# Second stage of an adaLN block with routed experts: where four quotients, their spreads, the row stores and the low halves are worked

## The reference

```python
h = layernorm(x) * (1 + ca) + sa
x = x + ga * attn(h)            # linear attention, 16 heads of 32
h = layernorm(x) * (1 + cb) + sb
x = x + gb * ffn(h)             # 8 experts, the 2 best of each token

def attn(x):                    # x: 2 x 4096 x 512
    q, k, v = relu(q), relu(k), v         # from x @ w_qkv.T
    vk = einsum('bhen,bhdn->bhed', pad_with_ones(v), k)
    out = einsum('bhed,bhdn->bhen', vk, q)
    out = out[:, :, :-1] / (out[:, :, -1:] + 1e-15)
    return out @ w_proj.T + b_proj
```

## Time and profile before

| what | value |
|---|---|
| time, median of 3 runs | 2205.16 us (2198.65 to 2208.55) |
| profiled execution | 2184.91 us, span 2183.0 us |
| second stage | about 600 to 995 us of the span |
| TensorE busy | 95% of the span |
| VectorE busy | 61% |
| GpSimd, ScalarE busy | 37%, 36% |
| granted clock of TensorE | 0.974 in the mean |

### The profile page before, as it was taken

The page is one execution under the profiler, slowest core; times in us unless marked ns, Lnnn a source line. Parts: engine busy times, 40 slices in busy tenths (PEclk is TensorE's granted clock), DMA queues, the critical chain, the costliest instruction groups (busy, mean ns, idle before and its releaser), DMA issues.

```text
span 2183.0 us, 42591 instructions
## 1 busy us (share of the span) xinstructions
PE 2070.9 (95%) x9416; PEld 1625.2 (74%) x9417; DVE 1322.6 (61%) x3179; ACT 794.0 (36%) x1493; POOL 804.6 (37%) x622
## 2 busy tenths in 40 slices
PE   6999999999979999983999999999999999999997
PEld 4888878888846665662788888888878778888885
DVE  6555564555267888874565656565655555565654
ACT  3444434444345665651222222222222222222222
POOL 4675656566414666653111111111111111111111
PEclk9999999999989999996999999999999999999998
DMA  8666565656545676766855558558775885865554
GB/s 275 241 213 208 168 207 167 207 171 207 183 141 187 228 268 221 275 233 223 238 130 126 129 125 247 124 132 232 181 189 129 264 209 129 237 133 126 130 108 79
DMA packets 293833, 404.89 MB, mean 185 GB/s; under 512 B 50648, under 2 KB 188888, under 8 KB 285920
## 3 DMA queue, kind: packets, MB, share of 16 engines
q1 hardware_dynamic: 166304, 259.74, 37.4%
q0 software_dynamic: 30096, 72.12, 16.0%
q10 hardware_dynamic: 97200, 70.82, 10.3%
HBM read 210.57 MB, written 191.98 MB: 184 GB/s over the span
## 4 chain that ended last, share of the span: by engine, by line
PE 48%; DMA 3%; issue 1%; SPq 1%; ACTq 1%; DVE 0%; ACT 0%; POOL 0%; DVEq 0%; POOLq 0%
PE bank L1753 48%; DMA act_rows<-hact 2%; ACTq L1041 1%; DMA out_rows<-orow,cur_tok 0%; DMA wbuf<-expert_split 0%; SPq L561 0%; DMA expert_rows<-rows,dest 0%; POOL expert_rows L752 0%; DVE x_t_lo L1616 0%; ACT x_t_hi L1023 0%; DVE act_t_lo L1633 0%; DMA meta<-expert_rows 0%; SPq L559 0%; DVE orow L1661 0%; POOL out_rows L773 0%
## 5 line engine op out<-in xcount | busy, mean ns | idle before, releaser
L1753 PE MATMUL bank<-wbuf,x_t_hi 128*128 x2160 | 681.1, 397 | 31.9 <-DVE x_t_lo L1616 29.0
L773 POOL DMA_INDIRECT out_rows<-orow,cur_tok x135 | 209.0, 1548 | 961.6 <-DVE orow L1661 727.8
L1753 PEld LDWEIGHTS bank<-wbuf,x_t_hi 128*128 128x128 f32 x2160 | 408.5, 189 | 129.6 <-issue 34.2
L1753 PE MATMUL bank<-wbuf,x_t_lo 128*128 x1080 | 427.6, 396 | 0.0
L1753 PE MATMUL bank<-wbuf,act_t_hi 128*128 x1080 | 341.0, 397 | 8.8 <-DVE act_t_lo L1633 8.8
L1622 DVE TENSOR_TENSOR hact<-bank,gact 128x512 f32<-128x512 f32 x135 | 93.3, 691 | 375.7 <-PE bank L1753 366.9
L1753 PEld LDWEIGHTS bank<-wbuf,act_t_hi 128*128 128x128 f32 x1080 | 204.4, 190 | 58.9 <-issue 11.3
L1753 PEld LDWEIGHTS bank<-wbuf,x_t_lo 128*128 128x128 f32 x1080 | 204.5, 189 | 47.9
L1753 PE MATMUL bank<-wbuf,act_t_lo 128*128 x540 | 214.3, 397 | 0.0
L1023 ACT ACTIVATE x_t_hi<-bank 128x512 fp32r<-128x512 f32 x135 | 80.9, 600 | 300.6 <-PE bank L1753 294.4
L1047 ACT ACTIVATE act_t_hi<-bank 128x512 fp32r<-128x512 f32 x135 | 80.8, 598 | 287.4 <-DMA arow<-act_rows 187.7
(11 more groups left out here) (225 smaller groups left out, 3865.0 us busy)
## 6 DMA issues: line engine op xcount, KB each, us to landing
wbuf<-expert_split SPq DMA_DIRECT2D x24, 1536.0 KB, 9.6
xrow<-expert_rows SPq DMA_DIRECT2D x540, 64.0 KB, 3.4
act_rows<-hact ACTq DMA_DIRECT2D x135, 256.0 KB
arow<-act_rows ACTq DMA_DIRECT2D x540, 64.0 KB
expert_split<-split_hi SPq DMA_DIRECT2D x32, 768.0 KB, 3.4
expert_split<-split_lo SPq DMA_DIRECT2D x32, 768.0 KB, 5.9
q_rows<-qf SPq DMA_DIRECT2D x16, 1024.0 KB, 6.8
qb<-q_rows SPq DMA_DIRECT2D x16, 1024.0 KB, 10.9
```

Source lines behind the costliest of these rows:

```text
L773: pool.indirect_dma_start(out=out, out_offset=bass.IndirectOffsetOnAxis(cur_tok[at][:, 0:1], 0), in_=orow[at % 2][:, :], in_offset=None, c ...
L1753: last = mm(dst, stationary(a, f), moving(b, f), start=(first and k == 0), stop=(k == parts * n - 1))
```

## The change

- `onf` has four buffers, and the four spreads of a group lie in four banks: `D_B`, `R_B` and the two of `RB_B` (group 0 keeps two). TensorE makes all four spreads together after `project(1)`; VectorE makes all four divisions together after `normed(1)`, ahead of `residual(2)`.
- `logits` now wait for division 0 and `turn_logits` for division 1 of the next group. `turn_logits` is put in after three of the twelve products of `project(3)`, `denominators` go ahead of `rank`.
- GpSimd makes low halves 0 and 1, VectorE low halves 2 and 3, after `residual(2)`. `number_rows` goes ahead of the scatter and waits for all four tiles of the scatter of g-2.
- VectorE starts a group with `recip`, then `residual(0)`, and `rms_var` comes after it. The router's small instructions, to `destinations`, go ahead of `centred(3)`.
- ScalarE starts a group with `off_squared(0)`, ahead of `rms_seed`; the squares of tiles 0 and 1 go ahead of `on_hi`, and `logits_out` stands between the third and the fourth.
- `x1` is stored tile by tile, each after its residual, with a semaphore for each tile.

The buffers, banks and SyncE:

```diff
-    onf = [sb(ph2, f"onf{i}", [P, GT], F32) for i in range(2)]
+    onf = [sb(ph2, f"onf{i}", [P, GT], F32) for i in range(HG)]
+    RB_OF = [[*RB_B, *RB_B], [D_B, R_B, *RB_B]]
...
-            sp.wait_ge(s_x1, TPG * (g + 1))
-            sp.dma_start(group_rows(out, g), x1[:, :, :]).then_inc(s_x1st, 16)
+            for t in range(TPG):
+                sp.wait_ge(s_x1, TPG * g + t + 1)
+                sp.dma_start(out[g * GT + t * P:g * GT + (t + 1) * P, :], x1[:, t, :]).then_inc(s_x1st[t], 16)
```

GpSimd:

```diff
         def number_rows(g, par):
+            for t in range(TPG):
+                at_least(pool, s_scat[t], SCAT * (g - 1))
...
             if has(g, 1):
-                for j in range(HG):
+                for j in range(HG // 2):
                     low_on(g + 1, 1 - par, j)
+            number_rows(g, par)
             if g:
                 scatter(g - 1, 1 - par)
-            number_rows(g, par)
```

ScalarE:

```diff
         def group2(g, par):
+            off_squared(g, 0)
             if before_it:
                 rms_seed(g - 1)
-            off_squared(g, 0)
...
             off_squared(g, 1)
             seed2(g, 0)
-            if more:
-                on_hi(g + 1, 1 - par, 0)
-                on_hi(g + 1, 1 - par, 1)
...
             square(g, 0, par)
+            square(g, 1, par)
+            if more:
+                for j in range(HG - 1):
+                    on_hi(g + 1, 1 - par, j)
             if before_it and more:
                 logits_out(g - 1)
+            if more:
+                on_hi(g + 1, 1 - par, HG - 1)
             off_squared(g, 2)
-            square(g, 1, par)
-            if more:
-                on_hi(g + 1, 1 - par, 2)
-                on_hi(g + 1, 1 - par, 3)
```

VectorE (quotients and order):

```diff
         def divide(g, par, j):
-            at_least(dve, s_onlo, HG * g + j - 1)
-            tt(onf[j % 2][:, :], RB_B[j % 2][:, :], qb[par][:, j, :], ALU.mult).then_inc(s_on, 1)
+            at_least(dve, s_onlo, HG * g)
+            tt(onf[j][:, :], RB_OF[min(g, 1)][j][:, :], qb[par][:, j, :], ALU.mult).then_inc(s_on, 1)
+        def low_on(g, par, j):
+            dve.wait_ge(s_onhi, HG * g + j + 1)
+            tt(on[par][1][:, j, :], onf[j][:, :], f32(on[par][0][:, j, :]), ALU.subtract).then_inc(s_onlo, 1)
...
         def group2(g, par):
+            if not last:
+                recip(g + 1)
+            residual(g, 0, par)
             if router:
                 rms_var(g - 1)
-            residual(g, 0, par)
+            residual(g, 1, par)
...
             normed(g, 1, par)
+            if not last:
+                for j in range(HG):
+                    divide(g + 1, 1 - par, j)
             residual(g, 2, par)
             if not last:
-                divide(g + 1, 1 - par, 2)
-                divide(g + 1, 1 - par, 3)
+                for j in range(HG // 2, HG):
+                    low_on(g + 1, 1 - par, j)
...
+            centred(g, 2)
             if now:
                 renorm()
                 places(g - 1)
                 scaled()
-            var2(g, 1)
-            if now:
                 renorm_recip()
                 places_chosen()
+                next_places()
+                weights(1 - par)
+                destinations(1 - par)
+            centred(g, 3)
+            var2(g, 1)
```

TensorE:

```diff
         def spread(g, j):
-            at_least(pe, s_on, HG * g + j - 1)
+                at_least(pe, s_on, j - 1)
+            else:
+                pe.wait_ge(s_on, HG * (g - 1) + j + 1)
+            if g and j == 1:
+                at_least(pe, s_ranku, g - 2)
...
         def logits_of(g, a, b):
-                pe.wait_ge(s_dene, min(g + 3, NG))
+                pe.wait_ge(s_on, min(HG * (g + 2) + 1, HG * NG))
...
         def turn_logits(g):
+            pe.wait_ge(s_on, min(HG * (g + 2) + 2, HG * NG))
...
             if has(g, 1):
-                spread(g + 1, 0)
-                spread(g + 1, 1)
+                for j in range(HG):
+                    spread(g + 1, j)
...
             if before_it:
                 logits(g - 1)
-            spread(g + 1, 2)
-            spread(g + 1, 3)
+                project(g, par, 3, between=lambda: turn_logits(g - 1), at=TPG - 1)
...
-            if before_it:
-                turn_logits(g - 1)
-            project(g, par, 3)
+            if has(g, 2):
+                denominators(g + 2, par)
             if before_it:
                 rank(g - 1)
-            if has(g, 2):
-                denominators(g + 2, par)
```

More of the change, by code:

```diff
@@ L294, in build @@
         sem("kvp_ready"), sem("kvp_hi_ready"), sem("kvp_lo_ready"), sem("sel_ready"))
-    s_q2, s_x2, s_x1st = sem("q_back"), sem("x_back"), sem("x1_stored")
+    s_q2, s_x2, s_x1st = sem("q_back"), sem("x_back"), [sem(f"x1_tile{t}_stored") for t in range(TPG)]
     s_den, s_aden, s_rec0, s_dene, s_rec, s_rb, s_on = (
@@ L1456, in group2 @@
             turn.begin(g, ROUTE_STEPS if router else 0)
+            if not last:
+                recip(g + 1)
+            residual(g, 0, par)
             if router:
                 rms_var(g - 1)
-            residual(g, 0, par)
+            residual(g, 1, par)
             if router:
                 rms_seed_squared(g - 1)
-            if not last:
-                recip(g + 1)
-            if router:
                 rms_seed_error()
-            residual(g, 1, par)
             mean(g, 0)
@@ L1471, in group2 @@
                 rms()
-            if not last:
-                divide(g + 1, 1 - par, 0)
-                divide(g + 1, 1 - par, 1)
             var2(g, 0)
@@ L1498, in group2 @@
             now = router and not last
-            centred(g, 2)
             if now:
                 exp_chosen(g - 1)
-            centred(g, 3)
+            centred(g, 2)
             if now:
@@ L1506, in group2 @@
                 scaled()
-            var2(g, 1)
-            if now:
                 renorm_recip()
                 places_chosen()
+                next_places()
[3 more added lines that the diff above has]
+            var2(g, 1)
             seed_squared(g, 1)
-            if now:
-                weights(1 - par)
             seed_error(1)
-            if now:
-                next_places()
-                destinations(1 - par)
             rstd2_of(1)
@@ L1534, in _ @@
         recip(0)
[L1535 to L1538 removed]
         divide(0, 0, 0)
         divide(0, 0, 1)
[L1542 removed]
+        low_on(0, 0, 0)
         divide(0, 0, 2)
[L1544 removed]
+        low_on(0, 0, 1)
         divide(0, 0, 3)
[L1546 to L1547 removed]
+        low_on(0, 0, 2)
+        low_on(0, 0, 3)
         keep_ksums(1, H2_B[1])
@@ L1746, in _, with product @@
         turn(0, 3)
-        def product(dst, parts, n, stationary, moving, first=True, between=None):
+        def product(dst, parts, n, stationary, moving, first=True, between=None, at=3 * FC // 2):
             k = 0
@@ L1754, in product @@
                     k += 1
-                    if between and k == parts * n // 2:
+                    if between and k == at:
                         between()
@@ L1871, in spread @@
                 pe.wait_ge(s_sel, 3 + NBLK)
-            at_least(pe, s_on, HG * g + j - 1)
+                at_least(pe, s_on, j - 1)
[3 more added lines that the diff above has]
+                at_least(pe, s_ranku, g - 2)
             heads = slice(j * BLK, (j + 1) * BLK)
-            mm(RB_B[j % 2][:, :], less_sel[heads, :], rec[heads, :], start=True, stop=True).then_inc(s_rb, 1)
+            mm(RB_OF[min(g, 1)][j][:, :], less_sel[heads, :], rec[heads, :], start=True, stop=True).then_inc(s_rb, 1)
         def project_sums(b, a):
@@ L1904, in rank, with project @@
             last.then_inc(s_rank, 1)
-        def project(g, par, t, between=None):
+        def project(g, par, t, between=None, at=3 * FC // 2):
             b = batch_of(g)
@@ L1915, in project @@
             product(dst, 3, FC, lambda a, f: on[par][a][:, f, t * P:(t + 1) * P],
-                    lambda k, f: kvp[k][:, b, f, :], first=False, between=between).then_inc(s_y, 1)
+                    lambda k, f: kvp[k][:, b, f, :], first=False, between=between, at=at).then_inc(s_y, 1)
         def turn_h2(g, par, t):
@@ L1970, in group2 @@
                 logits(g - 1)
-            spread(g + 1, 2)
-            spread(g + 1, 3)
-            if not before_it:
+                project(g, par, 3, between=lambda: turn_logits(g - 1), at=TPG - 1)
+            else:
                 for a in range(3):
                     project_sums(1, a)
-            if before_it:
-                turn_logits(g - 1)
-            project(g, par, 3)
+                project(g, par, 3)
+            if has(g, 2):
+                denominators(g + 2, par)
             if before_it:
                 rank(g - 1)
-            if has(g, 2):
-                denominators(g + 2, par)
             if not before_it:
```

28 lines of the change are left out of this document (11 added, 17 removed).

## The result

The change makes the kernel slower: 2220.3 us in the median against 2198.7 for the kernel before in the same series of runs, ratio 1.008, 95% interval 1.0047 to 1.0113. A second series with the changed kernel unaltered gave 2214.0 against 2201.7, 1.0048 (1.0024 to 1.0072). The ratios are those of the record for each series; they are not the quotients of the medians beside them (1.0099 and 1.0056 here). I had forecast 2200 and a range to 2216.

What follows compares the result with a forecast made beforehand. Second-stage loops of VectorE and TensorE were both taken as nearly closed. VectorE's 21.35 us a group against 21.65 saves 4.2 us over 14 groups, plus 1 us for steadier clock: 5 us, from 2205.2 to 2200, range 2182 to 2216.

Steps and rivals of the forecast that it cites:

- The sum of matmul time stays 19.75: TensorE, second stage: matmuls are moved, none added, so busy time per group stays 19.75 us.
- 0.8 for `logits` and 0.5 for `turn_logits`: TensorE's new waits per group: 0.8 us for division 0, 0.5 us because `logits_out` stands behind three `on_hi` on ScalarE.
- its loop closes in 19.75 and 1.3, 21.05: covered, by 0.3: TensorE's matmuls plus its two new waits make 21.05 us a group, 0.3 under VectorE's loop.
- Rival 3: Two short TensorE waits bring half-clock stretches in each group: loop 22.55 us, 13 us more, 2218; chance 0.08.
- VectorE's loop: VectorE's instructions per group, counted from residual 3: 20.95 us, plus 0.4 for scatter landing, 21.35.
- The two low halves: New on VectorE: they and GpSimd's two exclude each other; by that rule the pair costs VectorE 2.4 us, undisturbed 1.2.
- The landing: VectorE's `normed(1)` waits for scattered rows of two groups ago: new wait 0 to 0.5 us a group, 0.4 taken.
- rival 2: Tile 1's scatter lands as late as before; `normed(1)` waits 1.1 to 1.9 us, total 2211 to 2222; chance 0.15.
- `rank`'s wait: TensorE's wait for VectorE's `mkb` before `rank` nearly goes; 0.5 to 1 us appears before `logits`.
- rival 4: No change: the time won at `mkb` turns up at `logits`; loop within 0.15 us of 21.65, 2203 to 2207; chance 0.17.
- Groups 0, 1 and 15: Edge groups of the second stage: groups 0 and 15 gain and lose below 1 us; group 1 not mentioned.

Runs made afterwards that it cites:

- a_turn_first: Changed kernel with the transposes of tiles 2 and 3 ahead of the four spreads on TensorE: 2182.96 us, 0.9955 of before.
- a_pool_lows: Changed kernel with all four low halves on GpSimd, none on VectorE: 2195.18 us, 1.000 of before.
- a_tf_pool: Changed kernel with transposes of tiles 2 and 3 ahead of the four spreads and all four low halves on GpSimd: 2184.38 us, 0.9921 of before.
- a_whole_store: Changed kernel with a group's `x1` rows stored in one transfer, not by tiles: 2209.74 us, 1.008 of before.
- a_tf_ws: Changed kernel with transposes of tiles 2 and 3 ahead of the four spreads and `x1` stored whole: 2198.87 us, 0.9987 of before.
- a_fill: Changed kernel with five more useless matmuls of 512 columns ahead of the logits: 2205.87 us, 1.0028 of before.
- a_pool_fill: Changed kernel with all four low halves on GpSimd and five more useless matmuls ahead of the logits: 2203.76 us, 1.0015 of before.
- a_div_first: Changed kernel with divisions 0 and 1 back ahead of `var2(0)` on VectorE: 2214.32 us, 1.0038 of before.
- a_nudge: Changed kernel with one extra one-column activation on ScalarE behind the exponentials: 2214.54 us, 1.0054 of before.
- a_spread22: Changed kernel with spreads 2 and 3 put back behind the logits: 2217.07 us, 1.0099 of before.
- a_mid: Changed kernel with the transposes of tiles 2 and 3 between spreads 0, 1 and spreads 2, 3: 2187.28 us, 0.9949 of before.

## Why the prediction was wrong

- **The step that failed** is the one on TensorE, twice. "The sum of matmul time stays 19.75" left out that the four spreads, issued in one go on four row groups, run in the time that two took; a group at full clock is 18.83 us busy. Under a loop of VectorE of much the length that I had worked out, the waits that I put at 0.8 for `logits` and 0.5 for `turn_logits` were therefore 2.1 and 0.65. And "its loop closes in 19.75 and 1.3, 21.05: covered, by 0.3" priced these waits as idle time under VectorE's cover, when they cost clock.
- **Rival 3 is what happened**, given 0.08 and 2218. Its mechanism was right; its price was taken from before's groups at 0.92, 1.5 us, when the changed kernel's 5.2 us a group at half speed took 2.6. Nine of the twelve half-speed stretches stand behind one long wait at the logits, three behind a second one at `turn_logits`. My evidence against it, a wait of 0.74 us that left the clock alone, was too short a wait to tell. The trace of before had the longer ones: of its seven waits of 1.5 us or more ahead of `rank` in groups 2 to 14, five (1.53, 1.57, 1.69, 2.44 and 2.52 us) were followed by a half-speed stretch 0.9 to 1.9 us later, two (1.59 and 1.68) were not. Here the shortest, from the kernel before: a wait, and then products at 0.63 us that take 0.39 at full clock.

```profile
871.67 0.18 PE L1901 MATMUL bank<-mkb,before 128*128 128x8 bf16 x1 [1.53 <-DVE mkb L1391]
...
874.22 0.63 PE L1753 MATMUL bank<-kvp_hi,on_lo 128*128 128x512 f32 x1
...
877.32 0.39 PE L1753 MATMUL bank<-kvp_lo,on_hi 128*128 128x512 f32 x1
```

- **VectorE's loop**, 21.35 worked out, came out near the mark: 21.23 in a_turn_first, where the clock is out of play, and 21.2 by the estimate in the changed kernel. In part that is luck, since terms that were off cancelled. The idle time before both `var2` of a group was 0.7 (1.1 in a_turn_first), not 1.9; in the changed kernel VectorE waited 2.1 us a group for TensorE's projections and 0.9 for `on_hi` in its place. The two low halves together took 2.2 us in a_turn_first against the 2.4 that I had for them, but not as a pair that shuts each other out throughout: in each group one took 1.56 us beside GpSimd's and the other 0.68 without. Taken off VectorE they gave back 0.6 us a group (a_pool_lows), with the transposes first 0.16 (a_tf_pool), so VectorE's chain is not alone in setting the group.
- **The landing**: forecast 0 to 0.5 a group, measured 0.66 by the profile's own account, 0.83 before. All idle time before the normed rows is 1.12 a group, and was 1.06. That the stores by tiles help is right, by 0.8 us of this idle time (a_whole_store and a_tf_ws); rival 2 did not occur.
- **`rank`'s wait** is gone, as said, and came back at the logits, as rival 4 had it.
- **Groups 0, 1 and 15**: "below 1 us" for groups 0 and 15 and nothing for group 1 were 2.9, 2.1 and 4.7 us in our favour; group 1 had waited 1.3 and 2.3 us at `logits` and `turn_logits`, and lost clock (0.88 in 650 to 678; now 1.00).
- **What stays open**: why ScalarE's copies of tiles 2 and 3 start 3 us late in the changed kernel, a_fill, a_pool_fill, a_div_first and a_nudge, and on time in the other variants, some of which have the same order around them. The semaphore updates of the transposes and of tile 2's projection are what comes late. It is not the scatter's timing: in a_pool_lows and a_whole_store groups have their scatter within 0.1 us of where it stands to the transposes in the changed kernel. It is not needed for the loss, since a_whole_store and a_spread22 have it not and are as slow. But it has a part: late copies make the logits' way back late, and the second wait, 1.2 us or so at `turn_logits`, and the half-speed stretch that follows it stand almost only in kernels with late copies. What it costs by itself was not isolated. Also open is why equal waits of 1.5 to 2.9 us lose the clock in one group and not in the next.

## What to carry to other kernels

Work that is moved out of TensorE's way makes its next wait longer, and a wait isn't free just because another engine is the bound: read the clock column of the windows beside each wait, and price the wait at both clocks. The longest waits of the old kernel tell more than the shortest. If slack can't be avoided, split it over two places well apart: with 2.1 us ahead of the logits and 0.65 soon behind them a group took 2.5 us more than with 1.2 and 0.8 us that lay 6 us apart. Two waits only 3 to 4 us apart lost the clock often enough (three times in the changed kernel's groups 2 to 14). Before reckoning a move as "no work added", look at how the moved instructions run when they stand together.

## What the runs showed of the hardware

- Four matmuls of 32 rows on the four row groups, twice, take 1.14 us when issued together, as long as two of them twice (1.13).
- Stretches at 1.2 GHz of 3.4 to 10.2 us began between 0.6 us ahead of the end of a TensorE wait of 1.8 us or more at the logits and 1.6 us behind it (the waits of over 3 us in the changed kernel: at their end), or, 3.4 us long, 0.7 to 2.3 us behind a second wait of 0.8 to 1.3 us at `turn_logits` that followed a first of 0.4 to 1.9 us after 3 to 4 us. In groups 2 to 13 of all the traces no shorter wait at the logits lost the clock by itself, but ahead of `rank`, in the kernel before, waits of 1.53, 1.57 and 1.69 us did; single waits of up to 2.9 us kept it now and then.
- The same subtraction of VectorE (`low_on`, two tiles in SBUF) took 676 to 689 ns where it did not overlap with GpSimd's `low_on`, and 1.53 to 1.70 us where it did, in a_turn_first and a_mid.
- An engine can be released 4 us after the work that it waits for has ended by the profile (900.84 above against transposes that were through by 896.74, with the semaphore's update at 900.82), in six of the seventeen traces (the kernels named above) and not in the others.
